# Sixteen-head local attention on one Trainium2 core: values projected and weighed per head, in small array tiles

## The reference, cut to what matters

```python
qkv = x @ Wqkv                       # 128 -> 3 * 1024
q, k, v = split(qkv)                 # 16 heads of 64
q = rope(l2norm(q) * q_scale); k = rope(l2norm(k) * k_scale)
# windows of 32 queries, each with its own 32 keys and the 32 before
sim = einsum('bhwie,bhwje->bhwij', bq, bk2) * 8
attn = softmax(where(mask, -max, sim))
out = einsum('bhwij,bhwje->bhwie', attn, bv2)
x = out @ Wo + x                     # 1024 -> 128
x = ffn(x) + x
```

## Time and profile before

| | us |
|---|---|
| median of 3 runs (4336.21 to 4341.24) | 4340.46 |
| the profiled execution: its own time | 4337.86 |
| the profiled execution: span, first to last instruction | 4336.0 |

### The profile page before, as it was taken

How to read it: one execution, slowest core, us unless ns; L and a number is a source line. 1 busy time by engine, 2 the same in 40 slices (tenths; PEclk the granted TensorE clock), 3 DMA queues, 4 the chain that set the end, 5 groups by cost and what they waited for, 6 DMA issues and landing times.

```text
span 4336.0 us, 101314 instructions
## 1 busy us (share of the span) xinstructions
PE 3859.4 (89%) x30950; PEld 2929.2 (68%) x31328; DVE 3273.3 (75%) x5635; ACT 3104.5 (72%) x7150; POOL 2502.3 (58%) x2247
## 2 busy tenths in 40 slices
PE   6999997899997999988999979999889999789998
PEld 4666665677765777756777657777567776577776
DVE  6877776788866888667888668887678886678876
ACT  4777776777766777757777667777577776677775
POOL 1222223777746777646777457776477774577763
PEclk8999998999998999999999999999999999999999
DMA  2111111000000000010000000000100000000002
GB/s 76 40 30 30 40 30 29 1 0 0 0 26 2 1 0 0 1 26 2 0 0 0 27 1 1 0 0 1 26 1 0 0 0 27 1 1 0 0 1 65
DMA packets 53261, 52.86 MB, mean 12 GB/s; under 512 B 13574, under 2 KB 40452, under 8 KB 51972
## 3 DMA queue, kind: packets, MB, share of 16 engines
q1 hardware_dynamic: 52996, 49.77, 4.4%
HBM read 28.77 MB, written 4.19 MB: 8 GB/s over the span
## 4 chain that ended last, share of the span: by engine, by line
PE 42%; issue 24%; ACT 17%; DVE 14%; POOL 2%; ACTq 1%; DVEq 0%; SPq 0%; DMA 0%; POOLq 0%
PE bank L357 33%; ACT sb_area L668 9%; DVE sb_ssq L1105 6%; ACT sb_area L777 4%; DVE sb_smax L1116 3%; PE bank L416 3%; PE bank L503 2%; PE bank L561 2%; PE bank L532 1%; POOL sb_area L1333 1%; ACT sb_lnb L789 1%; ACT sb_lnb L786 1%; DVE sb_xs_lo L1073 1%; DVE sb_area L1093 1%; DVE sb_nmx L1012 1%
## 5 line engine op out<-in xcount | busy, mean ns | idle before, releaser
L668 ACT ACTIVATE sb_area<-bank 128x512 f32<-128x512 f32 (+4 forms) x3029 | 1569.7, 553 | 515.3 <-PE bank L357 340.2
L357 PE MATMUL bank<-sb_area 128*64 128x64 f32 (+4 forms) x16624 | 1291.6, 274 | 95.9 <-ACT sb_area L668 57.2
L1093 DVE TENSOR_TENSOR sb_area<-bank,sb_rots 128x1024 f32<-128x1024 f32 x768 | 939.0, 1225 | 524.5 <-ACT sb_area L777 521.2
L1308 POOL TENSOR_TENSOR sb_area<-sb_area,sb_rn 128x512 f32<-128x512 f32 x768 | 785.3, 1044 | 713.2 <-ACT sb_rn L793 713.2
L1294 POOL TENSOR_TENSOR sb_area<-sb_area 128x512 f32<-128x512 f32 x768 | 970.6, 1274 | 149.1 <-DVE sb_area L1093 147.3
L357 PEld LDWEIGHTS bank<-sb_area 128*64 128x64 f32 (+2 forms) x16624 | 852.4, 152 | 202.4 <-issue 141.4
L357 PE MATMUL bank<-sb_area,sb_wvo 128*128 128x256 f32 x3072 | 728.3, 381 | 3.1 <-DVE sb_xT L1151 3.1
L357 PE MATMUL bank<-sb_wqk_hi,sb_xs_hi 128*128 128x512 f32 x768 | 398.1, 518 | 242.0 <-DVE sb_xs_lo L1073 236.6
L357 PEld LDWEIGHTS bank<-sb_area,sb_wvo 128*128 128x128 f32 x3072 | 555.0, 190 | 78.3 <-issue 12.8
L777 ACT ACTIVATE sb_area<-bank 128x512 f32<-128x512 f32 x768 | 461.3, 601 | 118.8 <-PE bank L357 113.5
L503 PE MATMUL bank<-sb_ident,sb_area 128*128 128x128 f32 x3072 | 491.4, 283 | 36.8 <-ACT sb_area L668 32.7
(11 more groups left out here) (105 smaller groups left out, 5269.2 us busy)
## 6 DMA issues: line engine op xcount, KB each, us to landing
sb_xwin<-sb_p SPq DMA_DIRECT2D x256, 64.0 KB, 2.0
sb_area<-in_Wqkv SPq DMA_DIRECT2D x7, 1024.0 KB, 5.6
sb_area<-in_WvT SPq DMA_DIRECT2D x7, 512.0 KB, 7.4
sb_wo_bd<-in_Wo SPq DMA_DIRECT2D x14, 256.0 KB, 8.3
sb_area<-in_x SPq DMA_DIRECT2D x4, 512.0 KB, 5.8
sb_area<-in_x SPq DMA_DIRECT2D x8, 256.0 KB, 2.7
x_plus_causal<-sb_area SPq DMA_DIRECT2D x8, 256.0 KB, 2.3
out<-sb_area SPq DMA_DIRECT2D x8, 256.0 KB, 3.5
```

Of the source, the lines that this page charges most:

```text
L357: return nc.tensor.matmul(o, a, b, start=start, stop=stop, skip_group_check=True)
L668: return nc.scalar.activation(o, i, ACT.Copy)
L1093: tt_(t12[:, c % 2, :, :].rearrange("p u (h d) -> p u h d", h=8), src, bc(rots[:, tt, s, :, :], [P, 2, 8, D], 2), ALU.mult).then_inc(S["ro ...
L1308: pt_(qn[:, c, :].rearrange("p (h d) -> p h d", h=8), qsum[:, c % 2, :].rearrange("p (h d) -> p h d", h=8), r, ALU.mult).then_inc(S["qn"], 1)
```

## The change

Values are projected for each tile, 1024 columns, like q and k: `project_values(wp)` is three more f32r matmuls of 512 columns in each half, behind `score`. It writes `tbank`, the bank that `turn_p` also writes, so each of the two waits for ScalarE's copy of the other. ScalarE copies the values to `vt` (`projected_values`, one 128x512 copy in each half). The key windows of even queries straddle two 64-row halves, so two SBUF-to-SBUF DMAs per tile (4 KB rows, 128 in all, issued by SP) write a copy shifted by 32 rows, `vsh`.

`weigh()` is called once a step, in the second half, for the whole tile at lag 3: 64 matmuls, each with a loaded operand of 64 rows x 64 columns (a head's values) and 32 moving columns, in four array tiles of 64x64 in turn; the first is 128 columns wide. `score(h2)` takes one head of each pair at a time: 32 matmuls of 64 rows x 32 loaded columns and 64 moving ones, in four column tiles in turn, all on the same 64 rows. Queries stay whole (`qT`), so `turned_qk` is one copy.

`project_out` has 8 matmuls for two tiles, each for two heads, against the plain `Wo`: four in the first half of even steps, four in the second half of odd ones. `LAG` is 5. `windows`, `join_weights` and their copies are gone, `weighed` makes two copies a step and not four. `update` stands in VectorE's second half, ahead of `rests_of_tile`, and `shift_early` waits for the scaled q and k in place of the outputs. The weights to split are 6 x 512 columns and not 4.

```diff
-OUT_PARTS = (((6, 3), (5, 1)), ((5, 2), (4, 0)))
-LAG = 6
+OUT_PARTS = ((5, 1), (4, 0))
+LAG = 5
...
+                    def project_values(wp):
+                        if not (v := behind(t, i, part, 0)):
+                            return
+                        tt, bt = v
...
+                        pe.wait_ge(S["ptev"], g_of(i) * 8 + (2 * (t - 3) + wp + 1 if t >= 3 else 0))
...
+                        split3(tbank[:, :], xs_hi[:, tt % 2, :], xs_lo[:, tt % 2, :], wqkv_hi[:, w], wqkv_lo[:, w])\
+                            .then_inc(S["vproj"], 1)
...
-                        for g in range(HP):
-                            for x in range(2):
-                                hp, w = 2 * (g // 2) + x, wp + 2 * (g % 2)
+                        for a in range(4):
+                            for w2_ in range(2):
+                                w = a % 2 + 2 * w2_
                                 k0 = tt * P + w * WIN
-                                m = mm(sbank[64 * x:64 * x + 64, g * 64:(g + 1) * 64],
-                                       qbd[:, tt % 2, hp, w, :, :].rearrange("p a b -> p (a b)"),
-                                       kT[:, hp, k0:k0 + 2 * WIN], False, x == 1 and g == HP - 1)
+                                for cg in range(4):
+                                    hp = 4 * (a // 2) + cg
+                                    m = mm(sbank[32 * cg:32 * cg + 32, (2 * a + w2_) * 64:(2 * a + w2_) * 64 + 64],
+                                           qT[r, tt % 2, hp, w * WIN:(w + 1) * WIN], kT[r, hp, k0:k0 + 2 * WIN],
+                                           False, a == 3 and w2_ == 1)
...
+                        for a in range(4):
+                            values = vt[:, tt, :] if a % 2 else vsh[:, tt % 2, :]
+                            for cg in range(4):
+                                hp = 4 * (a // 2) + cg
+                                for w2_ in range(2):
+                                    keys = slice(64 * w2_, 64 * w2_ + 64)
+                                    for h2 in range(2):
+                                        h = 2 * hp + h2
+                                        if h == 0 and a == 0 and w2_ == 0:
+                                            mm(ybank[0][:, 0:WIN], values[keys, 0:2 * D], pT[keys, 0, 0:WIN])
+                                            continue
+                                        m = mm(ybank[w2_][64 * h2:64 * h2 + 64, hp * 64 + (a % 2) * WIN:hp * 64 + (a % 2 + 1) * WIN],
+                                               values[keys, h * D:(h + 1) * D],
+                                               pT[keys, h2, a * P + cg * WIN:a * P + (cg + 1) * WIN])
...
+                        for hp in range(4 * k, 4 * k + 4):
+                            m = mm(mbank[:, 0:256], wo[:, hp, :], ysb[:, hf, :, hp * 64:(hp + 1) * 64],
+                                   hp == 0, hp == HP - 1)
...
                         project(2 * wp + 1)
                         score(wp)
-                        if wp == 0:
-                            windows()
-                        weigh(4 - wp, 1 - wp)
+                        project_values(wp)
+                        if wp == 1:
+                            weigh()
                         turn_qk(2 * wp + 1)
                         project_out(wp)
-                    join_weights()
...
-                            dve.wait_ge(S["oo"], (l + 1) * (2 * B))
+                            dve.wait_ge(S["qn"], (l + 1) * (16 * B) + 6)
```

More of the change, by code:

```diff
@@ L78, in shape_constants @@
     first = ok & (key[None] >= WIN)
-    lmask = np.stack([np.tile(np.where(np.concatenate([m, ok], 1), 0.0, MASKED), (1, HP // 2)) for m in (first, ok)], 1)
+    lmask = np.stack([np.tile(np.where(np.concatenate([m, ok, ok, ok], 1), 0.0, MASKED), (1, 2)) for m in (first, ok)], 1)
     tri = np.where(np.arange(P)[None] <= np.arange(P)[:, None], 0.0, MASKED)
@@ L156, in build @@
         xn_all = take(NTOK)
[L157 removed]
+        wqkv_raw = take(3 * INNER)
         w1, w2 = take(2 * FF), take(3, C)
@@ L529, in turn_p @@
                         pe.wait_ge(S["pn"], m_ + 2)
-                        pe.wait_ge(S["ptev"], m_)
+                        values = min(t, 2 * TT) * 2 + (wp if t < 2 * TT else 0) if part == 2 else 2 * t + wp
+                        pe.wait_ge(S["vev"], g_of(i) * 8 + values)
+                        if part == 2 and t >= 2 * TT:
+                            pe.wait_ge(S["ptev"], m_)
                         for j in range(4):
@@ L761, in g_of @@
                         return l * B + bt
-                    def joined_weights():
-                        if part or t >= 4:
-                            return
-                        act.wait_ge(S["wvo_mm"], 4 * l + t + 1)
-                        copy(wvo[:, 4 * t:4 * t + 4, :], mbank[:, :].rearrange("p (a b) -> p a b", a=4))\
-                            .then_inc(S["wvo_ready"], 1)
                     def square(c):
@@ L846, in windows, with weighed @@
                         g = g_of(bt) * 4 + tt
-                        act.wait_ge(S["xwt"], g + 1)
-                        if not (part == 0 and t - 1 < TT):
-                            act.wait_ge(S["yy"], g * 4 - 10)
-                        copy(xw[:, tt, :, :], rbank[:, 0:256].rearrange("p (w c) -> p w c", w=2)).then_inc(S["xwev"], 1)
+                        act.wait_ge(S["vproj"], g * 2 + wp + 1)
+                        if not (part == 0 and t < 3):
+                            act.wait_ge(S[f"vshift{(tt + 1) % 2}"], 32 * (2 * g_of(bt) + (tt - 3) // 2 + 1))
+                            act.wait_ge(S["yy"], g - 1)
+                        copy(vt[:, tt, wp * 512:(wp + 1) * 512], tbank[:, :]).then_inc(S["vev"], 1)
+                    def weighed():
+                        if not (v := behind(t, i, part, 4)):
+                            return
+                        tt, bt = v
+                        act.wait_ge(S["yy"], g_of(bt) * 4 + tt + 3)
+                        act.wait_ge(S["oo"], g_of(bt) * 2 + tt // 2)
+                        copy(ysb[:, tt // 2, 2 * (tt % 2), :], ybank[0][:, :]).then_inc(S["yev0"], 1)
+                        copy(ysb[:, tt // 2, 2 * (tt % 2) + 1, :], ybank[1][:, :]).then_inc(S["yev1"], 1)
                     for wp in range(2):
@@ L1081, in load_next @@
                         if v := behind(t, i, part, -1):
-                            load_tile(*v, part == 0 and t + 1 < 2, not (part == 0 and t + 1 < TT))
+                            load_tile(*v, part == 0 and t + 1 < 2)
                     def rotate(c):
```

203 lines of the change are left out of this document (80 added, 123 removed).

## The result

| | before | after |
|---|---|---|
| median of four runs, us | 4338.34 | 4466.9 (4462.27 to 4474.32) |
| ratio | | 1.0298 [1.028, 1.0316] |
| profiled execution: own time, span, us | 4337.86, 4336.0 | 4474.32, 4472.5 |

The account below looks back on a forecast made before the run. TensorE was taken as the bound, 14.54 us of work in a 15.23 us step, VectorE's chain 0.55 us behind. Terms -73 - 12 - 55 + 9 + 20 = -111 on 4337.86 gave 4227, forecast 4230 us, range 4150 to 4620.

Parts of the forecast that it names:

- What the edits cost on the array: TensorE's step, part by part: scores unchanged, weighing +2.2, values +1.56, work from 14.54 to 14.16 us.
- The largest rival: Array instructions cannot start closer than 29 ns: TensorE 17.9 us a step, 4805 us (4615 by the skill's rule); chance 0.23.
- Weighing by twos: Rival: the weighing runs only two tiles at a time, scores four; 16.4 us a step, 4535 us; chance 0.15.
- Who is late next: Waits in the full step: odd steps 14.96 us by TensorE, even 14.56 by VectorE, mean 14.76 against 15.23, -73 us.
- the rival in which the step doesn't fall: ScalarE's copy and VectorE's update waits take the whole gain; only the drain pays, about 4305 us; chance 0.13.
- Code: Instruction fetch at returns of TensorE's longer loop body: 2.30 us each if not kept, 0 to +69 us, taken as +20.
- steps and ramp, the clock left out: Full steps -0.47 us each on 156, -73 us, and the ramp -2 a layer, -12 us.
- drain: End of each layer: deviations 29 us after TensorE's drain begins instead of 38.2; -9 us a layer, -55.
- between two layers, and the rest: Weights: two more 512-column subtractions on VectorE, +1.4 us, seven times, about +9 us.

Follow-up runs that it names:

- the written-out kernel: The changed kernel with TensorE's loop over the windows written out, so no return on TensorE inside a layer: 4363.38 us, ratio 1.0056.
- the run with one filler: The changed kernel with TensorE's loop written out and one thrown-away matmul in odd steps' wait ahead of the second half's values: 4285.84 us, ratio 0.9892.
- `xs_lo` first: The changed kernel, TensorE's loop written out, output group ahead of the values, VectorE's subtraction for `xs_lo` ahead of the output's addition: 4212.78 us, 0.9711.
- the output ahead: The changed kernel, loops kept, with the second half's output group moved ahead of the second half's values: 4393.06 us, ratio 1.0124.
- both edits: The changed kernel with TensorE's loop written out and the second half's output group moved ahead of its values: 4229.4 us, ratio 0.9753.
- 1118 us above: The changed kernel, loop written out and output ahead, with small matmuls reordered so neighbours use the same tile instead of taking turns: 6781.8 us.

## Why the prediction was wrong, step by step

**What the edits cost on the array: right.** Scores 1.10 us a pass, weighing 2.33 for 2.2, values 0.8 to 0.9 a group for 0.78, outputs as priced. The odd step from 1447.52 to 1462.93 us, less its 1.30 of waiting, is 14.11 us of work, forecast 14.16. The largest rival, a limit of starting at 29 ns or at the 25 ns of the Trainium skill (TensorE: Matmul & The Clock Gate, "Wait — 56ns, not 53.3ns?"), did not come: 1.10 / 64 = 17 and 2.33 / 128 = 18 ns from start to start, over four tiles in turn, less than the page's floor. Weighing by twos did not come either.

**Who is late next: right in kind, too short in size.** The odd steps' wait for ScalarE's copy was forecast at 0.8 us, from 8.9 to 9.7 after the step's start. In the written-out kernel TensorE waits 0.26 at the transposes ahead of it and 1.04 at the values, which start 961.18 - 951.02 = 10.2 us after the step's start. By TensorE's own starts the even steps of the run with one filler take 14.4 to 14.6 us, as forecast (14.56), and the odd ones 15.6 where 14.96 was forecast. With the waits' own length alone (that run, mean 15.12 over 156 full steps, where it was 15.21 before) the steps don't fall by 0.47 us but by 0.1, which is near the rival in which the step doesn't fall. Against the forecast this is 52 us of the 31 x 6 distances. Moving the output into the wait brings the 14.76 back (14.87, and 14.70 with `xs_lo` first).

**What wasn't in the sum at all: the clock behind the wait.** I took every duration at the level of before, whose loop shows 1.00 throughout although TensorE waits 0.55 us a step in it. That these waits do no harm was taken over without a word, and it isn't so for a longer wait behind the scores: 35 of 78 were followed by the lower level. From the kernel with the loop written out to the one with a filler the distances shrink by 90 us.

**Code: the mechanism right, the size wrong.** The term was 0 to +69 and taken at +20, 2.30 us a return from VectorE's stall between two layers, less what slack and queued work would hide. TensorE's own stall is 3.5 us, nothing of it is hidden, since the whole array is behind it, and it lowers the clock: at 29 of 30 returns a lower stretch begins. Returns and what follows them are worth 91 us in the distances (all steps of the changed kernel against those of the kernel with the loop written out), more than the upper bound of 69. Where the waits are gone (the output ahead, with and without the loop) they are worth 147, so how the loss is shared between the two causes depends on which is taken away first.

The sum against the profiled executions (spans 4472.5 - 4336.0 = 136.5 us, with both edits 4227.2 - 4336.0 = -108.8):

| term | forecast | in the changed kernel | with both edits |
|---|---|---|---|
| steps and ramp, the clock left out | -85 | -33.1 | -72.2 |
| lower clock behind the waits | 0 | +90.2 | 0 |
| returns and the clock behind them | +20 | +91.1 | 0 |
| drain | -55 | -17.1 | -42.5 |
| between two layers, and the rest | +9 | +5.4 | +5.8 |
| sum | -111 | +136.5 | -108.9 |

The first two rows of the changed kernel are split by the run with one filler, which has four lower stretches left, some 11 us; by so much the first may be lower and the second higher.

**Drain: nearly right, and partly hidden by the clock.** From the last full step's first rotation to the first deviation it was 51.0 us; it is 44.3 to 54.7 now, with 61 us at the lower level in the six of them, and 43.0 to 45.2 with both edits, with 7. That is 7.1 us a layer less, forecast 9. There the deviations start 29.9 us after TensorE's drain begins, forecast 29, before 38.2 (VectorE's and TensorE's timelines of that kernel):

```profile
1228.33 1.49 DVE L1044 TENSOR_TENSOR sb_area<-sb_area,bank 128x512 f32<-128x512 f32 x2 [0.87 <-issue]
```

```profile
1198.47 0.63 PE L499 MATMUL bank<-sb_ident,sb_area 128*128 128x128 f32 x4 [0.78 <-ACT sb_area L675]
```

So the sum of 4227 us fits another kernel than the one that was made: the one with both edits, 4229.4. That it fits so closely is luck: that kernel has no returns, so the +20 has no place in it, and its steps and drain saved 25 us less than forecast. The rivals that I gave for slower, the array's starts and the weighing by twos, did not come. What came was a small term of the sum, the returns, and one that wasn't in it, the clock behind a wait.

## What to carry to other kernels

An edit that makes many small instructions out of few large ones has a second price beside the array's: count the instructions in the body of each hardware loop, and where the body grows past what the trace shows to be kept, price every return with the stall of that engine and a few us of lower clock, or write the loop out. And when an edit opens a wait on TensorE beside groups of small tiles, price it with the clock that may follow (here about 90 us for 78 waits of about 1 us in the six layers, of which 35 were followed by the lower level), and look for a full-array group that can be moved into it: that adds no work, and here it saved the clock and 39 us of waiting besides (-72.2 against -33.1).

## What the runs showed of the hardware

- Four tiles in turn start an f32 matmul with its own load every 17 to 18 ns; one tile after itself every 50 (64x32) to 57 ns (64x64).
- The granted clock falls with TensorE busy throughout, where only one 64x64 tile works (1118 us above, and 191 of 192 weighings of that run).
- Waits of 0.86 to 1.21 us between the scores and the values were followed by the lower level in 35 of 78 places; the 78 waits for `xs_lo` of up to 1.20 us in the kernel with both edits, ahead of a step's full-array groups, in none. The place alone doesn't decide it: in the two kernels that leave out part of the weighing, 11 of the 84 waits for `xs_lo` of over 0.8 us were followed by it, all 11 of them 1.23 to 1.70 us long. What picks the 35 of 78 isn't shown.
- TensorE's code comes at 19 to 42 packets of 16 KB in 250 us without costing time in straight code that the runs could show; a return to a body that isn't kept costs 3.0 to 5.0 us of standing still, at about 110 as at 160 KB.
